# Gated delta attention plus MoE in one kernel: K's and Q's right halves decayed by one VectorE product instead of two

## What is computed

```python
q = short_conv(x @ Wq.T, wq_conv).reshape(B, T, H, D)      # likewise k, v; 4 taps, then silu
q, k = scale ** 2 * _rmsn(q, EPS_QK), scale * _rmsn(k, EPS_QK)
g = -jnp.exp(A_log)[None, None, :, None] * jax.nn.softplus(a_logits + dt_bias)
beta = jax.nn.sigmoid(x @ Wb.T)
def step(S, inputs):
    q_t, k_t, v_t, g_t, b_t = inputs
    S = S * jnp.exp(g_t)[..., None]
    kv = jnp.einsum('bhd,bhdv->bhv', k_t, S)
    delta = b_t[..., None] * (v_t - kv)
    S = S + k_t[..., None] * delta[:, :, None, :]
    return (S, jnp.einsum('bhd,bhdv->bhv', q_t, S))
```

## Time and profile before

| | |
|---|---|
| median of 3 runs | 6594.8 us |
| the profiled execution's own time | 6597.35 us |
| its span, first to last instruction | 6595.6 us |
| mean granted TensorE clock | 0.982 |
| TensorE busy | 5985.2 us, 91% |
| VectorE busy | 4296.0 us, 65% |
| ScalarE busy | 3226.7 us, 49% |
| GpSimd busy | 1967.6 us, 30% |

### The profile page before, as it was taken

How to read it: one execution, slowest core, us unless ns; L and a number is a source line. 1 busy time by engine, 2 the same in 40 slices (tenths; PEclk the granted TensorE clock), 3 DMA queues, 4 the chain that set the end, 5 groups by cost and what they waited for, 6 DMA issues and landing times.

```text
span 6595.6 us, 129491 instructions
## 1 busy us (share of the span) xinstructions
PE 5985.2 (91%) x38912; PEld 4897.0 (74%) x38912; DVE 4296.0 (65%) x11329; ACT 3226.7 (49%) x6704; POOL 1967.6 (30%) x2752
## 2 busy tenths in 40 slices
PE   7998989999989989898999999898989999899999
PEld 5777777777777777777777777777777777755555
DVE  5766666666666666666666666766666666655555
ACT  4555555555555555555555555555555555411111
POOL 3333333333333333333333333333333333300000
PEclk9999999999999999999999999999999999999999
DMA  2000000000000000000000000000000000000000
GB/s 72 17 17 17 14 17 16 14 17 17 14 17 16 14 17 17 14 17 17 13 17 17 15 17 18 16 14 17 17 14 17 16 14 17 28 7 13 10 10 13
DMA packets 55225, 112.63 MB, mean 17 GB/s; under 512 B 5088, under 2 KB 38112, under 8 KB 54496
## 3 DMA queue, kind: packets, MB, share of 16 engines
q1 hardware_dynamic: 54624, 105.42, 5.0%
HBM read 97.01 MB, written 8.39 MB: 16 GB/s over the span
## 4 chain that ended last, share of the span: by engine, by line
issue 39%; PE 34%; POOL 17%; ACT 6%; DVE 2%; POOLq 1%; DVEq 0%; ACTq 0%
POOL kl L314 8%; PE bank L1134 7%; PE bank L1089 6%; PE bank L939 4%; PE bank L1106 3%; PE bank L1144 3%; POOL e_sb L340 2%; POOL e_sb L343 2%; POOL TT L333 2%; ACT L512 2%; POOL T L329 2%; PE bank L957 2%; PE bank L984 2%; ACT vs L442 1%; PE bank L969 1%
## 5 line engine op out<-in xcount | busy, mean ns | idle before, releaser
L314 POOL TENSOR_TENSOR kl<-kl,tot 128x256 f32<-128x256 f32 x768 | 501.8, 653 | 1990.2 <-PE bank L939 1990.2
L939 PE MATMUL bank<-kq,kl 128*128 128x128 f32 x6144 | 867.4, 285 | 217.8 <-DVE AT L638 204.3
L939 PEld LDWEIGHTS bank<-kq,kl 128*128 128x128 f32 x6144 | 760.6, 194 | 270.4 <-issue 215.9
L957 PE MATMUL bank<-T,lx 128*128 128x64 f32 x6144 | 780.3, 270 | 0.0
L922 PE MATMUL bank<-xT,par 128*128 128x512 f32 x1536 | 779.2, 604 | 0.8 <-ACT gaT L397 0.8
L979 PEld LDWEIGHTS bank<-lx,TT 128*128 128x128 f32 x5120 | 630.6, 191 | 195.2 <-ACT lx L416 134.5
L957 PEld LDWEIGHTS bank<-T,lx 128*128 128x128 f32 x6144 | 756.5, 194 | 0.0
L979 PE MATMUL bank<-lx,TT 128*128 128x64 f32 x5120 | 681.0, 276 | 55.4 <-ACT lx L416 35.9
L969 PE MATMUL bank<-ident,T 128*128 128x128 f32 x3072 | 486.2, 281 | 170.2 <-DVE T L660 170.2
L434 ACT ACTIVATE W<-bank 128x128 f32<-128x128 f32 x512 | 141.8, 277 | 965.1 <-PE bank L1020 965.1
L628 DVE TENSOR_TENSOR kq<-kq,tot 128x256 f32<-128x256 f32 x1536 | 583.0, 421 | 0.0
(11 more groups left out here) (165 smaller groups left out, 12969.0 us busy)
## 6 DMA issues: line engine op xcount, KB each, us to landing
par<-params_dram SPq DMA_DIRECT2D x128, 519.0 KB, 3.5
wo<-wo_dram SPq DMA_DIRECT2D x128, 128.0 KB, 2.0
xall<-x_dram SPq DMA_DIRECT2D x16, 512.0 KB, 3.8
out_dram<-xall SPq DMA_DIRECT2D x16, 512.0 KB, 2.9
lx<-ffn_dram SPq DMA_DIRECT2D x1, 3456.0 KB, 11.8
wfa_sb<-wfa_dram SPq DMA_DIRECT2D x1, 128.0 KB, 2.1
wga_sb<-wga_dram SPq DMA_DIRECT2D x1, 128.0 KB, 2.1
wb_sb<-wb_dram SPq DMA_DIRECT2D x1, 8.0 KB, 1.8
```

The lines of the kernel that those rows point to most:

```text
L314: pool.tensor_tensor(halves(kl[:, :], h)[:, :, 0, :], src, totr.broadcast_to([P, SEQ // (2 * h), h]), ALU.mult).then_inc(s["kl_ready"], 1)
L939: ins = pe.matmul(dst[:, :, n], chunk(left, n), right[:, :, n, :, 1, :], start=True, stop=True)
L957: ins = pe.matmul(b_x[:, n * HALF:(n + 1) * HALF].rearrange("p (m h) -> p m h", h=h), chunk(LT[l], n), halves(chunk(T, n), h)[:, :, 0, :], ...
```

## The change

`kq_update(l)` multiplied K's right halves (part 0) and then Q's (part 1), 256 elements per partition each, by the same broadcast of totals. Now one product covers both parts: 512 elements per partition, with the factor's access repeated over the parts with stride 0. At level 0 the factor is `a`, at later levels `tot`. `kq_ready` is raised once per call, as it was.

```diff
                     totl = tot_view(pB, l).rearrange("p (m two) -> p m two", two=2)[:, :, 0:1]
-                    for part in range(2):
-                        view = halves(chunk(kq[pB], part, SEQ), h)[:, :, 1, :]
-                        ins = dve.tensor_tensor(view, view, totl.broadcast_to([P, m, h]), ALU.mult)
+                    view = kq[pB][:, :].rearrange("p (q m two h) -> p q m two h", q=2, two=2, h=h)[:, :, :, 1, :]
+                    ins = dve.tensor_tensor(view, view, totl.unsqueeze(1).broadcast_to([P, 2, m, h]), ALU.mult)
                     ins.then_inc(s["kq_ready"], 1)
```

## The result

The changed kernel takes 6369.7 us (median of 4 runs, 6366.7 to 6374.4) where the kernel before takes 6596.3 over its runs of the same comparison: a ratio of 0.9655, 95% interval 0.9639 to 0.9672. It is faster by 226 us. I had forecast 110.

The account below looks back on a forecast made before the run. TensorE, busy 91% of the span, was taken as the bound, so VectorE savings pay only where it waits. From 6597.35 us, 83.7 for the level-0 stall and 26.5 for instructions (110) gave 6487; range over the cases 6455 to 6548.

Parts of the forecast that it names:

- The hold at level 0: At level 0 GpSimd's L329 holds VectorE's second product by 0.845 us in 99 steps; merging saves 83.7 us.
- GpSimd's delay: At level 0 L329 and L333 end later, L333 by 0.09 us; L314 of level 1 keeps 0.11, so no cost.
- Levels 1 to 6: One instruction fewer saves 0.07 us per level; only levels 1 and 3 count here, the others have slack.
- the sum: Whole kernel: 83.7 us for the stall plus 26.5 for instructions at levels 0, 1 and 3, 110 us in all.
- (a): Later in the step another engine gives back a third to two thirds of level 0's gain: 6515 to 6543; chance 0.12.
- (b): At level 0 L329 gets the read path ahead of the merged product or in its middle: about 6585; chance 0.10.
- (c): At each level the merged access streams slower, 512 elements taking 1.06 us: 6672, slower than before; chance 0.05.

Follow-up runs that it names:

- two_inits_first: The kernel before, with GpSimd's start values of T and TT moved ahead of the level-0 update of kl: 6612.3 us, ratio 1.0022.
- one_from_1: The changed kernel with two products again at level 0, one product at levels 1 to 6: 6495.1 us, ratio 0.9838 to the kernel before.
- two_shift64: The kernel before with 64 tiny copies added on VectorE once, ahead of all loops: 6525.3 us, ratio 0.9892.
- one_shift50: The changed kernel with 50 tiny copies added on VectorE once, ahead of all loops: 6432.8 us, ratio 0.9757 to the kernel before.
- one_at_0: The changed kernel with one product at level 0 alone, two products again at levels 1 to 6: 6456.5 us, ratio 0.9786 to the kernel before.

## Why the prediction was wrong

**The hold at level 0** was right in cause and size. The second product takes over 1.2 us in 99 steps of the kernel before, the number that I had worked out; the single one takes 0.68; the copy comes 0.92 earlier, L329 ends 0.26 to 0.27 later, L333 runs at 1.04, and TensorE keeps 0.21 of wait (I had 0.17). That GpSimd's delay costs nothing at level 1 held: L314 of level 1 starts 1.23 behind TensorE's level 1 as before. `two_inits_first` shows that L329 is what holds the product.

**Levels 1 to 6** were right in place. The waits before L1007 and the L968 behind level 3, to be laid beside the earlier trace rows:

```profile
2896.02 0.49 PE L1007 MATMUL bank<-S,kq 128*128 128x128 f32 x2 [0.17 <-DVE S L690]
...
2907.18 0.66 PE L968 MATMUL bank<-ident,T 128*128 128x128 f32 x4 [0.55 <-DVE T L659]
```

0.23 became 0.17 and 0.61 became 0.55. `one_from_1` gives 0.19 per step for all six levels where I had 0.14; the 0.05 stays open. The ordinary step lost 1.10 and not 1.05, which over 128 steps would be 6 us. One new wait has come: at level 6 TensorE follows GpSimd's L314, where its products started at once in the kernel before.

```profile
2914.50 1.16 PE L938 MATMUL bank<-kq,kl 128*128 128x128 f32 x8 [0.15 <-POOL kl L314]
```

**The step that failed is the sum.** It took the eight steps of a sequence for six ordinary ones and two in which there was little to gain, and let it rest there: "one has the pair free (0.76)". I used that step as proof of L329's normal duration and didn't ask why its products came at 3046 when GpSimd was through by 3045. The trace had the answer, VectorE idle for 2.48 and 1.55 us with no releaser, and a step of 46.9 us. The sum then lacked a term, which it put at nothing without a reason: the second loading of VectorE's own code, by its place and length, which measured 71 us with what it does to TensorE's clock. The clock in the two long steps at a sequence's end, some 26 us by the account below, was missing too. None of the rivals had either. All three are out: nothing but the 0.15 at level 6 was given back later in the step (a), the product kept its turn (b), and 512 elements take 0.684 as forecast (c).

**Where the 226 went.** By `two_shift64`, which is the kernel before without the second loading: 71 us are the loading (the fourth steps from 46.9 to 42.5). A part of it is TensorE's clock. In the kernel before TensorE waits 4.09 us in that step, and at the end of the wait the granted clock falls to 0.50, the lower of its two levels (1.2 and 2.4 GHz), for 3.4 us. The windows of the wait and of that stretch (the clock is the third number from the end):

```profile
3043.90:3047.87 3.97, 0.03 (x1) 0.00 (x0) 2.25 (x8) 0.67 (x1) 0.87 (x1) 1.00 0.01 4
3047.87:3051.29 3.42, 3.27 (x15) 3.31 (x16) 0.54 (x2) 0.00 (x0) 0.74 (x1) 0.50 0.00 0
```

Summed over the 15 fourth steps (from VectorE's start of level 0 to the next one), 75 us stand at 0.50 in the kernel before and none in `two_shift64`. TensorE is busy in such a stretch, so about half of it is lost, by my estimate some 37 of the 71. In `one_shift50` TensorE waits only 2.39 in that step, the clock stays at 1.00 in 14 of 15, and the step is 2.1 longer, not 4.4. In `one_at_0` the wait is as short, 2.4, but the clock falls in all 15, and the step is 3.8 longer; why there and not in `one_shift50` stays open.

The other 155 are between `two_shift64` and the changed kernel. 110 are what I had summed up. The fourth steps, once they are on time, are ordinary ones and have the hold as well (114 held products in `two_shift64`, 99 in the kernel before): 15 x 0.92 = 14. The 0.05 by which an ordinary step lost more are 6. The remaining 25 are in the last two steps of a sequence, by the clock again. The step with the preparation lost 32 us in 16, where an ordinary one loses 1.1. Seven of the 16 lost 1.1 to 1.2 and have as many stretches at 0.50 as in `two_shift64`; seven lost 2.8 to 2.9 and have one stretch of 3.4 us fewer; one with two fewer lost 4.5, and one with one more got longer by 0.4. In the step ahead of it, in which the product isn't held, the time at 0.50 went from 58 us to 34, and in the preparation's from 61 to 34. Half of both differences is 26.

Over the whole span the mean clock is 0.982 before and 0.991 after. With two levels a mean of 0.982 means 2 x 0.018 x 6596 = 237 us at the lower one, and 0.991 means 115; half of the difference, some 60 of the 226 us, is my estimate for the clock. The low stretch shown stands behind a wait of TensorE, and TensorE waits less now; no run changes its waits and nothing else, so that this is the reason is argued, not shown.

## What to carry over

Ask for the reason of every irregular step before its numbers are used for anything: windows over whole iterations, side by side, show them, and idle time that no semaphore ended ("issue"), at the head of a loop, is a term of its own. A change in the number of instructions moves all code behind it, so a small edit can gain or lose 1% by where a loop's body falls; shifting the kernel before by a few dozen idle instructions tells such a gain from the edit's own. A wait of TensorE can cost more than its length where its clock falls, as in the fourth step here: read the granted clock of every long step. Two instructions on one engine that another engine can get in between are worth merging where a third waits behind them, and who starts first, here by 0.06 us, decides who pays.

## What the runs showed of the hardware

Instructions are loaded in packets of 8.2 KB on the queue whose count moved when VectorE's list alone was edited. With 128 instructions a packet, the second pass of a loop is free when its body touches three such pieces (up to 302 instructions here) and costs the step 2 to 4.5 us when it touches four (from 288; 41.4 to 43.5, and 42.5 to 46.9 with a fall of TensorE's clock in it). The Trainium skill, "Runtime: NRT & Kernel Launch", section "Instruction fetch mechanics", warns that a taken branch whose target isn't in the window of pages being held forces a load before execution goes on; the trace agrees, with 2.48 and 1.55 us of idle time in that step. The Trainium skill has in the same section blocks of 16 KiB and a window of two of them; the packets here are half as large, and the seven kernels fit either size.

A VectorE product with two inputs in SBUF keeps GpSimd's product waiting while it reads (0.27 and 0.53 us by my estimate), and not for its whole length: 0.21 with 256 elements and 0.48 with 512 (1.52 less 1.04), 0.27 more for 0.27 more of reading. GpSimd's product of 512 holds VectorE's for 0.85 (1262 ns less 416).

TensorE's granted clock fell to 0.50 for 3.4 us at the end of its wait of 4.09 us. With waits of 2.4 us at the same place it fell in `one_at_0` and stayed at 1.00 in 14 of 15 steps of `one_shift50`.
